# Three of sixteen scan states unturned: decays in PSUM from ScalarE, inputs in SBUF from GpSimd, and the first norms on ScalarE

## The reference: what is computed

```
x1 = x + attn(layernorm(x))          # attn: layernorm again, mamba, residual, gated feed-forward
y  = x1 + experts(layernorm(x1))     # 8 experts of rank 128, the best 2 weighted per token
```

```
dA = exp(dt[t,d] * A[d,s])
h[d,s] = h[d,s] * dA + dt[t,d] * B[t,s] * xc[t,d]
y[t,d] = sum over s of h[d,s] * C[t,s]
```

## Time and profile before

| | |
|---|---|
| median of 3 runs | 1325.81 us |
| the profiled execution's own time | 1326.64 us |
| its span, from the first to the last instruction | 1324.9 us |
| mean granted TensorE clock over the span | 0.986 |
| TensorE matmul, weight load | 1223.9 us (92%), 1052.6 us (79%) |
| VectorE | 1006.5 us (76%) |
| ScalarE | 1039.5 us (78%) |
| GpSimd | 1079.5 us (81%) |

### The profile page before, as it was taken

The page is one execution under the profiler, slowest core; times in us unless marked ns, Lnnn a source line. Parts: engine busy times, 40 slices in busy tenths (PEclk is TensorE's granted clock), DMA queues, the critical chain, the costliest instruction groups (busy, mean ns, idle before and its releaser), DMA issues.

```text
span 1324.9 us, 24291 instructions
## 1 busy us (share of the span) xinstructions
PE 1223.9 (92%) x7678; PEld 1052.6 (79%) x7678; DVE 1006.5 (76%) x1800; ACT 1039.5 (78%) x2506; POOL 1079.5 (81%) x820
## 2 busy tenths in 40 slices
PE   5677899999999999999999999999999999998988
PEld 3466688888888888788878878888887888787876
DVE  2597979788796978779687787969778796878733
ACT  4889988798887879878787887878888787877521
POOL 2589898898988888798888988889898888889631
PEclk8899999999999999999999999999999999999999
DMA  2411112021021202112111211211111121202010
GB/s 69 175 48 41 48 41 80 22 78 48 32 81 50 80 24 76 49 33 81 50 67 32 72 46 47 81 49 57 41 64 49 49 72 49 69 28 74 17 48 16
DMA packets 29063, 74.02 MB, mean 56 GB/s; under 512 B 3080, under 2 KB 15744, under 8 KB 26496
## 3 DMA queue, kind: packets, MB, share of 16 engines
q1 hardware_dynamic: 28928, 72.35, 16.4%
HBM read 63.56 MB, written 4.58 MB: 51 GB/s over the span
## 4 chain that ended last, share of the span: by engine, by line
PE 66%; DVE 10%; issue 6%; ACT 5%; DMA 3%; POOL 2%; DVEq 0%; ACTq 0%; SPq 0%; POOLq 0%
PE psx L1241 11%; PE psy L1260 11%; PE pst L1123 8%; PE psb L1117 7%; PE psb L1123 7%; DVE h L998 4%; PE pst L1117 4%; PE psf L1117 3%; PE psf L1209 2%; PE psf L1160 2%; PE psf L1149 2%; DMA cbc<-cw_scratch 2%; PE psb L1215 2%; ACT dA L807 1%; PE psf L1215 1%
## 5 line engine op out<-in xcount | busy, mean ns | idle before, releaser
L998 DVE TENSOR_TENSOR_SCAN h<-dA,state,psx 128x256 f32<-128x256 f32 x1024 | 682.4, 726 | 112.6 <-PE psx L1241 94.7
L577 POOL TENSOR_TENSOR hC<-h,bC 128x1024 f32<-128x1024 f32 x256 | 607.2, 2377 | 86.9 <-DVE h L998 80.3
L807 ACT ACTIVATE dA<-dt,neg_a 128x256 f32<-128x256 f32 x1024 | 434.1, 499 | 0.0
L1241 PE MATMUL psx<-ident,bxT 128*128 128x128 f32 x2048 | 306.0, 275 | 22.6 <-DVE h L998 16.0
L1241 PEld LDWEIGHTS psx<-ident,bxT 128*128 128x128 f32 x2048 | 244.9, 142 | 65.8 <-issue 28.0
L795 ACT ACTIVATE bxT<-uTs,BT 128x512 f32<-128x512 f32 x352 | 232.6, 715 | 69.1 <-PE psx L1241 67.6
L1260 PE MATMUL psy<-ident,hC 128*128 128x128 f32 x2048 | 266.2, 273 | 1.5 <-POOL hC L577 1.5
L1260 PEld LDWEIGHTS psy<-ident,hC 128*128 128x128 f32 x2048 | 233.9, 142 | 4.7 <-POOL hC L577 1.7
L561 POOL TENSOR_TENSOR bxT<-uTs,BT 128x1024 f32<-128x1024 f32 x80 | 152.2, 1902 | 24.8 <-PE psx L1241 24.8
L1117 PE MATMUL psb<-nT,w_ff_sb 128*128 128x256 f32 x496 | 121.8, 388 | 12.8 <-ACT yg L820 11.2
L1117 PE MATMUL pst<-eT,w_a_sb 128*128 128x256 f32 x448 | 107.9, 384 | 19.9 <-DVE cbc L1073 19.9
(11 more groups left out here) (165 smaller groups left out, 1601.5 us busy)
## 6 DMA issues: line engine op xcount, KB each, us to landing
bC<-bc_scratch SPq DMA_DIRECT2D x64, 512.0 KB, 3.8
cbc<-cw_scratch SPq DMA_DIRECT2D x15, 1024.0 KB, 4.8
xf<-in_x SPq DMA_DIRECT2D x16, 256.0 KB, 2.8
xk<-xn SPq DMA_DIRECT2D x16, 256.0 KB, 4.3
xb<-in_x SPq DMA_DIRECT2D x16, 256.0 KB, 4.3
out<-x SPq DMA_DIRECT2D x16, 256.0 KB, 2.2
w_in_sb<-in_w_in SPq DMA_DIRECT2D x1, 1024.0 KB, 5.2
w_ff_sb<-in_w_ff SPq DMA_DIRECT2D x1, 1024.0 KB, 5.8
```

The lines of the kernel that those rows point to most:

```text
L577: nc.gpsimd.tensor_tensor(hC[:, s % RC], h[:, ring(s)], bC[:, g % RINGG, s % G:s % G + 1, :].to_broadcast([P, NJ, T]), ALU.mult).then_inc( ...
L807: last = nc.scalar.activation(dA[:, s % RA, j, :], dt[:, n[1], j, :], ACT.Exp, scale=neg_a[:, j, s:s + 1])
L998: last = nc.vector.tensor_tensor_scan(h[:, r, j, :], dA[:, s % RA, j, :], psx[bx_bank(fill)][:, k, :], state[:, b, j, s:s + 1], ALU.mult, ...
L1241: last = nc.tensor.transpose(psx[bx_bank(fill)][:, k, j * P:(j + 1) * P], bxT[:, ring(s), j, c:c + P], ident[:, :])
```

## The change

States 0, 1 and 2 (DIRECT) are no longer turned. Their inputs are made by channels: GpSimd multiplies `u` (by channels in SBUF) by the B row of the state, broadcast over the partitions by a DMA into the new tile `bB`, and writes a slot of `bxT`. Their decays go into the PSUM banks `psx`, from ScalarE; VectorE scans with the decay in PSUM and the input in SBUF. TensorE's 24 transposes of these states and their six waits go. The ring `bxT` gets a fourth slot, and GpSimd's other states are 4, 6 and 8 only, so that ScalarE makes 3, 5, 7 and 9 to 15. State 3 is scaled, and its decays made, in `ready` 15.

`xn`, `xk` and the copy between them go. ScalarE makes the deviations with a negated mean (`minus`), GpSimd the product of both (`biases`, tiny), and the four columns are kept by a small DMA, `kept`. ScalarE then makes `un` in `enter` 15 with a scale and a bias per partition, and, in `back` 4, the first norm again from `xb` straight into `x1`; VectorE's sum in `back` 6 is made in place. The B rows are stored with the C rows, and the load of `bB` (three rows) is issued in `ready` 5; the late weights of the first step follow it. `skip` moves from `ready` 12 to `ready` 14.

The diff, cut to its core:

```
-RX = 3
+RX = 4
-POOL_STATES = (4, 6, 8, 14, 15)
+DIRECT = (0, 1, 2)
+POOL_STATES = (4, 6, 8)

 def made_at(s):
-    return (-2, -1)[s] if s < 2 else s - 3 if s < S - 1 else S - 3
+    return {3: -1, 14: 12, 15: 13}[s] if s in (3, 14, 15) else s - 3
+def decayed_at(s):
+    return {3: -1, 15: 13}[s] if s in (3, 15) else s - 3
+def direct_at(turn):
+    return {12: (0,), 13: (1,), 14: (2,)}[turn] if turn in (12, 13, 14) else ()

+        def scaled_free(eng, s, n):
+            k = s - RX
+            step_back = 0 if k >= 0 else 1
+            k += S * step_back
+            if k in DIRECT:
+                eng.wait_ge(scan_done, count(FILLS, n, HALVES * (k + 1) - FILLS * step_back))
+            else:
+                eng.wait_ge(bx_filled, count(TURNED, n, turned(k) + HALVES - TURNED * step_back))
```

SP queue:

```
             def load_x(m):
-                sp.wait_ge(xn_done, copied)
+                gone = value(count(1, m, 0))
+                sp.wait_ge(un_done, gone)
...
-                    sp.dma_start(bc_scratch[m[1]], bc[S:2 * S, :]).then_inc(bc_stored, 16)
+                    sp.dma_start(bc_scratch[m[1]], bc[:, :]).then_inc(bc_stored, 16)
             def ready(s, m):
+                if s == 5:
+                    sp.wait_ge(bc_stored, stored)
+                    sp.wait_ge(direct_done, scaled)
+                    sp.dma_start(bB[:, :, :], bc_scratch[m[1]][0:ND, :].partition_broadcast(P)).then_inc(b_loaded, 16)
                 if s == 8:
-                    sp.dma_start(xk[:, m[1]], xn[:, m[1]]).then_inc(xk_copied, 16)
+                    sp.dma_start(kept[:, m[1]], scales[:, m[1]]).then_inc(scales_kept, 16)
```

GpSimd, in `ready` behind u:

```
+                for k in direct_at(s):
+                    weigh_direct(k, m)
+            def weigh_direct(s, n):
+                if s == DIRECT[0]:
+                    pool.wait_ge(u_done, count(1, n, 1))
+                    pool.wait_ge(b_loaded, count(16, n, 16))
+                scaled_free(pool, s, n)
+                nc.gpsimd.tensor_tensor(by_channels(s), u[:, :, :], bB[:, s:s + 1, :].to_broadcast([P, NJ, T]), ALU.mult
+                                        ).then_inc(direct_done, 1)
```

ScalarE:

```
+            def scaled(dst, src, tab, k, m, done):
+                for j in range(SUB):
+                    last = nc.scalar.activation(dst[:, j, :], src[:, j, :], ACT.Identity, scale=tab[:, m[1], k, j:j + 1],
+                                                bias=tab[:, m[1], 2 + k, j:j + 1])
+                last.then_inc(done, 1)
             def enter(s, m):
+                if s == 15 and not is_last(m):
+                    norm_again(following(m))
             def ready(s, m):
-                if s >= 13:
-                    made(s - S, m)
+                if s == 15:
+                    made(-1, m)
+                    if not is_first(m):
+                        decay_direct(0, 0, m)
+            def decay_direct(s, part, n):
+                fill = HALVES * s + part
...
+                act.wait_ge(scan_done, count(FILLS, n, bx_before(fill) + 1))
+                for k in range(PAIR):
+                    j = PAIR * part + k
+                    last = nc.scalar.activation(psx[bx_bank(fill)][:, k, :], dt[:, n[1], j, :], ACT.Exp,
+                                                scale=neg_a[:, j, s:s + 1])
+                last.then_inc(direct_exp, 1)
             def main(s, n, part):
+                if part == 0 and s == 0:
+                    if not is_first(n):
+                        decay_direct(0, 1, n)
+                    decay_direct(1, 0, n)
+                if part == 0 and s == 1:
+                    decay_direct(2, 0, n)
+                if part == 1 and s in (0, 1):
+                    decay_direct(s + 1, 1, n)
             def back(s, m):
+                if s == 4:
+                    act.wait_ge(xb_loaded, count(16, m, 16))
+                    act.wait_ge(scales_kept, count(16, m, 16))
+                    act.wait_ge(x1x_done, count(1, m, 0))
+                    scaled(x1, xb, kept, 0, m, xn_done)
```

VectorE and TensorE:

```
+                if s in DIRECT:
+                    dve.wait_ge(direct_exp, count(HALVES * ND, n, fill + 1))
+                    decays, inputs = ((in_psum, by_channels(s)[:, j, :]) if s in DIRECT
+                                      else (dA[:, decay_slot(s), j, :], in_psum))
-                    nc.vector.tensor_tensor(x1[:, :, :], xk[:, b], psb[:, :, :], ALU.add).then_inc(x1_done, 1)
+                    nc.vector.tensor_tensor(x1[:, :, :], x1[:, :, :], psb[:, :, :], ALU.add).then_inc(x1_done, 1)
-                if s == 15:
-                    fill_bx(0, 0, m)
-                    fill_bx(0, 1, m)
-                if s + 1 < S:
+                if s + 1 < S and s + 1 not in DIRECT:
                     fill_bx(s + 1, part, n)
```

More of the change, by code:

```diff
@@ L231, in mamba_moe @@
         lnv = [sb(f"lnv{k}", [P, SUB]) for k in range(4)]
-        rstd = [sb(f"rstd{k}", [P, SUB]) for k in range(4)]
+        rstd = {k: sb(f"rstd{k}", [P, SUB]) for k in (2, 3)}
         eps2_c = sb("eps2_c", [P, 1])
@@ L782, in made @@
                 for k in range(S):
-                    if made_at(k) == turn and k not in POOL_STATES:
+                    if k not in DIRECT and made_at(k) == turn and k not in POOL_STATES:
                         weigh_u(k, n)
-                if turn + 3 < S and not (is_first(n) and turn < -1):
-                    decay(turn + 3, n)
+                for k in range(S):
+                    if k not in DIRECT and decayed_at(k) == turn:
+                        decay(k, n)
             def weigh_u(s, n):
-                if s == 0:
+                if s == ND:
                     act.wait_ge(BT_done, count(1, n, 1))
                     act.wait_ge(uTs_done, count(2, n, 2))
-                act.wait_ge(bx_filled, count(FILLS, n, HALVES * (ring_before(s) + 1)))
+                scaled_free(act, s, n)
                 for j in range(SUB):
-                    last = nc.scalar.activation(bxT[:, ring(s), j, :], uTs[:, n[1], j, :], ACT.Copy,
+                    last = nc.scalar.activation(by_tokens(s)[:, j, :], uTs[:, n[1], j, :], ACT.Copy,
                                                 scale=BT[:, n[1], j, s:s + 1])
@@ L799, in decay @@
             def decay(s, n):
-                if s == 0:
+                act.wait_ge(scan_done, count(FILLS, n, HALVES * (decay_before(s) + 1)))
+                for j in range(NJ):
+                    last = nc.scalar.activation(dA[:, decay_slot(s), j, :], dt[:, n[1], j, :], ACT.Exp,
+                                                scale=neg_a[:, j, s:s + 1])
+                last.then_inc(exp_done, 1)
+            def decay_direct(s, part, n):
+                fill = HALVES * s + part
+                if fill == 0:
                     act.wait_ge(dt_done, count(1, n, 1))
@@ L804, in decay @@
                         act.wait_ge(a_ready, 1)
-                act.wait_ge(scan_done, count(FILLS, n, HALVES * (s + 1 - RA)))
-                for j in range(NJ):
-                    last = nc.scalar.activation(dA[:, s % RA, j, :], dt[:, n[1], j, :], ACT.Exp,
+                act.wait_ge(scan_done, count(FILLS, n, bx_before(fill) + 1))
+                if is_first(n) and fill == 2:
+                    act.wait_ge(conv_tap, 2 * NJ * (TAPS - 1))
+                for k in range(PAIR):
+                    j = PAIR * part + k
+                    last = nc.scalar.activation(psx[bx_bank(fill)][:, k, :], dt[:, n[1], j, :], ACT.Exp,
                                                 scale=neg_a[:, j, s:s + 1])
-                last.then_inc(exp_done, 1)
+                last.then_inc(direct_exp, 1)
             def keep_state(s, n):
```

130 lines of the change are left out of this document (77 added, 53 removed).

## The result

The kernel after takes 1386.11 us, the median of 4 runs (1382.32 to 1388.2), against 1325.64 before (1324.79 to 1325.93): a ratio of 1.0448, 95% interval 1.0432 to 1.0464. I forecast 1362 and a range up to 1378: the direction was right, the time lies 8 us beyond the range. The profiled execution after took 1382.32 us, that before 1326.64: 55.7 us more.

A forecast was written before the change was run, and what follows sets the result against it. TensorE was taken to bound turns 7 to 14, TensorE and ScalarE both the rest. Twelve iterations at +3.1 (37 us), +1 for four others and -2 in the opening gave +36: 1362 us, range 1316 to 1378 (own forecast 1335 to 1376).

The forecast's parts named there:

- The sum over ScalarE up to `halo`: From TensorE's last fill of state 15 (the release) to the halo copy: -4.05 + 4.8 + 1.0 + 1.0 + 0.7 = +3.4 us.
- The delay arrives whole: From the halo copy in order through VectorE and TensorE to the cbc product, ScalarE's delay is passed on in full.
- The late part: Turns 7 to 14 of an iteration, where TensorE alone sets the pace; to stay at 41.9 us.
- the third rival: The cbc copy lands late behind bB and xf: +1 to +2 us an iteration more, 1375 to 1390 us; chance 10%.
- The banks: PSUM banks bind so tightly that scans of states 0 to 2 run one fill at a time; included in a 10% chance.
- A new wait: ScalarE's low copy, behind un and fills 1 and 2, ends at 6.7 instead of 4.6; eT at 9.1: 0.7 us more idling.
- +3.1 an iteration: Cost taken for each of twelve full iterations, within bounds of +1.0 to +5 us.
- The opening: Before the main loop: an earlier first scan, between 4.5 us saved and nothing; 2 us taken.
- TensorE's wait before the second hidden-layer matmuls: Wait for VectorE's cbc product at 375.83, said to grow from 1.2 to 6 or 7 us.
- VectorE's wait for `halo`: Wait at 363.03, 0.95 us before the change, said to become 3 us or more.
- The two rules: Skill texts: optimize the engine with highest occupancy first (TensorE, faster, 18%); PSUM is the lower-latency destination for an activation.
- the sum of +2.9: ScalarE's total up to the halo copy if each of the 12 exponentials into PSUM took 0.36 us.

The follow-up runs named there:

- run 11: Kernel after with only the first norm into x1 moved from back 4 to back 5, behind the halo copy; 1379.0 us, ratio 1.0396.
- run 4: Kernel before with only the norms moved (un, x1 on ScalarE; no xn, xk), all 16 states turned; 1341.46 us, ratio 1.0111.
- run 3: Kernel after with un, fill 0 and the decays of state 3 put ahead of bxT 3 in ScalarE's turn 15; 1345.08 us, ratio 1.0135.
- Run 1: Kernel after with 24 idle identity transposes on TensorE ahead of its wait for the low copy; 1367.07 us, ratio 1.0302.
- run 9: Kernel before with 18 of the 24 transposes an iteration left out and nothing added, inputs partly stale; 1324.47 us, ratio 0.9971.
- run 8: Kernel before, all 16 states turned, norms on ScalarE, four bxT slots, x1 in back 5; 1325.79 us, ratio 0.9983.
- run 10: Kernel after with un, fill 0, decays 3 ahead, x1 in back 5, plus 24 identity transposes before the low wait; 1353.55 us, ratio 1.0185.
- run 5: Kernel after with un, fill 0 and decays 3 ahead of bxT 3, and x1 moved to back 5; 1336.66 us, ratio 1.0071.

## Why the prediction was wrong in size and right in direction

**Right, by its own steps.** The sum over ScalarE up to `halo` was +3.4; measured +3.51. Within it: `low` over at 6.8 us after the release (forecast 6.7), `eT` at 9.30 (9.1), four exponentials into PSUM 1.59 (1.6), `un` and `x1` 0.98 and 0.99 (1.0 each). "The delay arrives whole" held wherever the distance from the release to `halo` was read: +3.51 gave +3.51, run 11's +2.55 gave +2.55, run 4's +1.72 gave +1.73, run 3's +1.0 gave +1.0. The late part stayed at 41.88 (41.9). GpSimd came out at -1.5 (-1.6). `cbc` decided in no full iteration: VectorE waited for that copy 7.9 us in 3 places, all behind the last full iteration (before, 11.6 us in 5 places, two of them in the long iterations), so the third rival falls. The banks did not bind either: ScalarE's decays into PSUM waited 1.5 us in all for scans.

**The step that failed: "A new wait", with its "0.7 us more of idling".** I worked out that `low` comes late and booked ScalarE's idle time before `eT` alone. I did not ask what TensorE does meanwhile: with its transposes gone and `low` late it stands still for 3.39 us, and behind that its clock is at 0.50 for some 3 to 7 us in eight of twelve iterations. I did expect TensorE to idle 6 or 7 us an iteration, at another place, and still the sum had no term for the clock. Run 1 prices it: 1386.11 less 1367.07, 19 us. Put on top of 1362 it would have been 1381.

**A second step was smaller than its rows.** I took +3.1 an iteration "between the 3.4 of the rows and the overlap I may have missed". Steady iterations lost 3.51. The mean without the clock was lower for another reason: the thirteen iterations sum to 1002.75 us before and to 1042.76 in run 1, 40.0 more or 3.08 each, since the four long ones of before (78.35 to 79.69) had up to 2.4 us of their own in them and those of run 1 (81.00 to 81.56) only up to 0.8. So 3.1 came out as a mean by luck. For run 1's profiled execution the whole difference is -2.7 before the first `low` projection, +40.0, and +0.9 behind the last, 38.2; I had +36.

**The opening** was forecast at -2 by an earlier first scan. The first `low` projection came 2.2 us earlier (115.04 against 117.27), but the first scan ran at 49.77, 2.3 later than in the earlier trace rows, behind VectorE's 7.11 us wait for `xf`. It had stood behind `xf` before too (a wait of 5.15 us, over at 46.49), so an earlier input could not have moved it. The number held by luck, the mechanism did not.

**Two signs were named wrongly.** I said that TensorE's wait before the second hidden-layer matmuls would grow from 1.2 to 6 or 7 us; it stayed at 1.20. The idle time of the early part did grow by 5.84 us, but in four earlier places, the first of them in front of the step sizes, where it costs clock. And VectorE's wait for `halo` grew to 1.96 us, not 3, because VectorE came to it 2.50 us later itself. Its waits on the way were 4.37 us in place of 3.02: 2.68 for the direct scans, hardly more than the 2.46 of the earlier trace rows, and a new 1.17 for GpSimd's `psel`, which needs ScalarE's `pr`:

```profile
601.89 1.39 DVE L1117 TENSOR_TENSOR_SCAN h<-psx,state,bxT 128x256 f32<-128x256 f32 x2 [2.19 <-ACT psx L904]
603.77 5.24 DVE L1117 TENSOR_TENSOR_SCAN h<-psx,state,bxT 128x256 f32<-128x256 f32 x8 [0.49 <-ACT psx L904]
...
618.48 0.17 DVE L1180 TENSOR_REDUCE den<-psel 128x2 f32<-128x16 f32 x1 [1.17 <-POOL psel L705]
...
624.25 2.43 DVE L1081 SCALAR_TENSOR_TENSOR acc<-psf,par,acc 128x255 f32<-128x255 f32 x6 [1.96 <-ACT halo L783]
```

**The two rules.** TensorE was 92% busy, and relieving it gave nothing in a steady iteration (run 9); the average hides that a longer ScalarE chain makes the early part longer, one for one. The Trainium skill, Perfetto Trace Analysis, "Identifying the Most-Contended Engine", says to optimize the engine with the highest occupancy first. Taken with the 92% of the matmuls, as I took it, the measurement decides against it here. I left out that the Trainium skill, in the same section, judges TensorE's headroom by its weight loads (or by the work it does against its peak) and not by its busy matmuls. The weight loads are 79% here, beside 81% for GpSimd and 78% for ScalarE, and single out no engine. A single record is shorter (464 ns against 501 for `dA`), but the exponentials still start 0.40 us apart, so the time that counts is the same. The Trainium skill, ScalarE: Activation LUTs, "Step-by-step: what each stage is for", has PSUM as the lower-latency destination: the record agrees, but the sum of +2.9 that I drew from it was not seen.

**What stays open.** Why 3.39 us of idling lowers the clock in some iterations and not in others; and what holds the iteration at 77.2 in run 8, where the release no longer does. There ScalarE, TensorE and VectorE hand over to each other with short waits from `low` to `cbc`. ScalarE takes 18.39 us from its `low` copy to the end of `halo`, 1.05 of them idle, which points to its chain again; but no run made that stretch shorter than before, so it isn't shown.

## What to carry to other kernels

Cut an iteration at the waits that end last and ask each part separately which engine's in-order chain fills it: work that is moved onto that chain cost its full length here, whatever another engine saved. When a change delays a result that TensorE waits for and takes away the work that covered the wait, price both the idle time and the clock behind it, and look for the idle time at the first wait in program order, not at the last. If the order must stay, filler on TensorE in that gap can win time back (19 us here; in run 10, where the gap was short, it cost time). Placing the new work ahead of the release won more (41 us, run 3), and `x1` behind the critical copy another 8 (run 5).

## What was unexpected of the hardware

TensorE's clock stood at 0.50 for some 3 to 7 us behind 3.39 us of idling in a kernel that is 87% busy, and cost 1.06 to 2.20 us an iteration; with 2.6 us of identity transposes in the gap it stayed at 1.00 in all twelve iterations behind the first. Activations into PSUM and into SBUF start equally far apart, 0.40 us for 128x256 f32, though the record into PSUM is 37 ns shorter.
